# Self-attention on one Trainium2 core: values of two pairs of heads projected together

## What is computed

```python
def _L0_attn_ref(x, Wq, Wkv, Wo, bo, rel_emb):          # x is already normed: (2, 1024, 256)
    q = (x @ Wq).reshape(b, n, h, d).transpose(0, 2, 1, 3)
    kv = x @ Wkv
    k, v = jnp.split(kv, 2, axis=-1)
    ...
    dots = jnp.einsum('bhid,bhjd->bhij', q, k) * scale
    dots = dots + _rel_bias(rel_emb, n)[None]
    attn = jax.nn.softmax(dots, axis=-1)
    out = jnp.einsum('bhij,bhjd->bhid', attn, v)
    out = out.transpose(0, 2, 1, 3).reshape(b, n, h * d)
    return out @ Wo + bo
```

## Time and profile before

| | |
|---|---|
| median of 3 runs | 2049.24 us (2044.33 to 2055.61) |
| the profiled execution | 2053.66 us, span 2051.9 us |
| self-attention loop, first to last scores' block | about 58 to 901 us of the span |
| PE / DVE / ACT / POOL busy, share of the span | 91% / 63% / 47% / 47% |
| mean granted clock of TensorE | 0.959 of full |

### The profile page before, as it was taken

The page is one execution under the profiler, slowest core; times in us unless marked ns, Lnnn a source line. Parts: engine busy times, 40 slices in busy tenths (PEclk is TensorE's granted clock), DMA queues, the critical chain, the costliest instruction groups (busy, mean ns, idle before and its releaser), DMA issues.

```text
span 2051.9 us, 52537 instructions
## 1 busy us (share of the span) xinstructions
PE 1871.6 (91%) x21476; PEld 1552.1 (76%) x21476; DVE 1301.8 (63%) x2932; ACT 973.9 (47%) x1984; POOL 967.1 (47%) x783
## 2 busy tenths in 40 slices
PE   7999999999999999987559489999999999988994
PEld 5677777777777777765447389999899999987873
DVE  6667676767676766647756565555565554556883
ACT  3666666666666666533136043334343443335451
POOL 2555555555555555545633733334234334435440
PEclk9999999999999999999869699999999999999996
DMA  6101020101230100234133520000220000220000
GB/s 246 50 19 47 19 78 19 50 19 70 101 129 19 50 12 12 70 133 130 47 135 126 155 78 13 23 13 13 79 80 26 19 18 18 85 73 16 15 14 16
DMA packets 74606, 119.85 MB, mean 58 GB/s; under 512 B 8392, under 2 KB 64464, under 8 KB 70992
## 3 DMA queue, kind: packets, MB, share of 16 engines
q1 hardware_dynamic: 69392, 105.31, 15.3%
q0 software_dynamic: 2560, 6.30, 1.1%
q10 hardware_dynamic: 2416, 4.88, 0.6%
HBM read 76.61 MB, written 39.85 MB: 57 GB/s over the span
## 4 chain that ended last, share of the span: by engine, by line
PE 41%; DVE 5%; POOL 3%; issue 2%; DMA 2%; ACT 2%; SPq 1%; POOLq 0%; DVEq 0%; ACTq 0%
PE psum L265 12%; PE psum L276 9%; PE psum L2019 4%; PE psum L2007 2%; PE psum L2511 2%; PE psum L1993 2%; PE psum L225 1%; PE psum L2545 1%; PE psum L1367 1%; PE psum L1350 1%; POOL b_yg L1484 1%; PE psum L246 1%; ACT e_pr L2650 1%; PE psum L1260 1%; PE psum L2520 1%
## 5 line engine op out<-in xcount | busy, mean ns | idle before, releaser
L774 POOL TENSOR_TENSOR a_sm<-a_sm,a_rsum 128x1024 f32<-128x1024 f32 x256 | 479.8, 1893 | 357.5 <-DVE a_rsum L808 355.1
L796 DVE CUSTOM_DVE_ANT_0 a_sm<-psum,a_strip 128x1024 f32<-128x1024 f32 x256 | 312.0, 1219 | 146.8 <-PE psum L628 146.8
L709 ACT ACTIVATE a_sm<-a_sm,a_mn 128x1024 f32<-128x1024 f32 x256 | 293.9, 1148 | 28.2 <-DVE a_mn L796 26.9
L714 ACT ACTIVATE a_pT<-psum 128x512 f32<-128x512 f32 x256 | 151.5, 592 | 273.1 <-PE psum L641 273.1
L641 PE MATMUL psum<-ident,a_sm 128*128 128x128 f32 x2048 | 275.2, 277 | 5.2 <-POOL a_sm L774 4.2
L641 PEld LDWEIGHTS psum<-ident,a_sm 128*128 128x128 f32 x2048 | 223.8, 140 | 62.7 <-issue 46.0
L656 PE MATMUL psum<-a_pT,a_V 128*64 128x256 f32 x2048 | 249.0, 385 | 0.6 <-ACT a_o L720 0.6
L656 PEld LDWEIGHTS psum<-a_pT,a_V 128*64 128x64 f32 x2048 | 136.1, 136 | 77.3 <-issue 22.1
L803 DVE COPY a_pT<-psum 128x512 f32<-128x512 f32 x256 | 174.8, 683 | 12.1 <-PE psum L641 4.9
L2103 ACT ACTIVATE g_val<-psum 128x512 f32<-128x512 f32 x64 | 38.0, 596 | 225.0 <-PE psum L2019 225.0
L628 PE MATMUL psum<-a_KH,a_QH 64*128 64x512 f32 x512 | 114.8, 445 | 2.5 <-DVE a_mn L796 2.5
(11 more groups left out here) (396 smaller groups left out, 3736.2 us busy)
## 6 DMA issues: line engine op xcount, KB each, us to landing
a_strip<-table SPq DMA_DIRECT2D x16, 960.0 KB, 6.7
oT<-a_o SPq DMA_DIRECT2D x64, 128.0 KB, 1.9
xs<-b_zeros SPq DMA_DIRECT2D x8, 1024.0 KB, 4.1
b_oT_in<-oT SPq DMA_DIRECT2D x7, 1024.0 KB, 5.9
y<-b_yb SPq DMA_DIRECT2D x23, 256.0 KB, 2.2
b_xs<-xs SPq DMA_DIRECT2D x23, 128.0 KB, 2.2
a_raw<-in_a_wqkv SPq DMA_DIRECT2D x7, 384.0 KB, 3.3
s_x<-in_x_rev SPq DMA_DIRECT2D x4, 512.0 KB, 8.0
```

Of the source, the lines that this page charges most:

```text
L709: a.activation(sm[:, st % RING, :], sm[:, st % RING, :], ACT.Exp, scale=-1.0, bias=mn[:, at:at + 1], accum_out=rsum[:, at:at + 1]).then_in ...
L714: a.activation(probs(st, 0), psum[:, 4, :].rearrange("p (k q) -> p k q", k=4), ACT.Copy).then_inc(sig("pT_act"), 1)
L774: g.tensor_tensor(sm[:, st % RING, :], sm[:, st % RING, :], rsum[:, at:at + 1].broadcast_to([P, T]), ALU.mult).then_inc(sig("scaled"), 1)
L796: v.tensor_tensor_reduce(out=sm[:, st % RING, :], in0=scores_banks(hl).rearrange("p c n -> p (c n)"), in1=strip[:, pair % 2, hl, qt * P:qt ...
```

## The change

Values of an even pair and of the odd pair after it are projected in one unit. The stationary operand is still a tile of tokens; the moving operand is the values' weights of both pairs side by side, 256 columns, and the three passes are accumulated in the same columns (12 matmuls of 256 columns, no 128-column ones, no second partial sum). ACT copies the even pair's columns into a buffer of its own, `Vs[0]`, which lies where the next stage's first slot will be loaded; DVE copies the odd pair's columns into `Vs[1]` (a copy where an addition was).

A block of an even pair has 8 units, one of an odd pair only its 4 k and q units. These are put at tiles 0, 2, 3 and 5 of the block before it; tiles 1, 4, 6 and 7 have no unit. `split(1)` is moved ahead of the loop, since the first v unit needs both pairs' weights, and its raw load ahead of the strips; the later splits and raw loads are moved to match.

```diff
-        Ws = [sb(f"W{r}", [P, 2, KC, 3 * P], F32R, lies=32) for r in range(2)]
+        W_pair = sb("W", [P, 2, 2, KC, 3 * P], F32R, lies=32)
+        Ws = [W_pair[:, r, :, :, :] for r in range(2)]
...
-        V = sb("V", [P, B, KT, P])
+        Vs = [nc.alloc_sbuf_tensor_at("a_V_even", [P, B, KT, P], F32, offset=early["wo_at"] + HP * D * 4), sb("V", [P, B, KT, P])]
...
-        parts = [("k", 0), ("k", 1), ("q", 0), ("q", 1)] + [("v", c) for c in range(KT // 2)]
-        NU = len(parts)
-        ACT_V = NU - 4
-        units = [(pair, b, what, c) for pair, b in blocks for what, c in parts]
+        both = [("k", 0), ("k", 1), ("q", 0), ("q", 1)]
+        parts = [both + [("v", c) for c in range(KT // 2)], both]
+        NU, NQK = len(parts[0]), len(both)
+        units = [(pair, b, what, c) for pair, b in blocks for what, c in parts[pair % 2]]
+        base = [sum(len(parts[pair % 2]) for pair, _ in blocks[:i]) for i in range(len(blocks) + 1)]
+        unit_at = {}
+        for i, (pair, _) in enumerate(blocks[1:]):
+            for u, n in enumerate(range(KT) if pair % 2 == 0 else (0, 2, 3, 5)):
+                unit_at[i * KT + n] = base[i + 1] + u
...
+        split_at = {2 * KT * (pair - 1 - pair % 2) + (KT if pair % 2 else 2): pair for pair in range(2, HP)}
...
+                load_raw(1)
                 load_strips(0)
-                load_raw(1)
                 load_strips(1)
...
-                    if g % 8 == 2 and pair + 2 < HP:
-
+                    if g % 8 == 2 and pair % 2 == 0 and pair + 2 < HP:
                         sp.wait_ge(sig("w_lo"), pair + 1)
                         load_raw(pair + 2)
+                        load_raw(pair + 3)
...
+                    if (what, c) == ("v", 0):
+                        pe.wait_ge(sig("w_lo"), pair + 1)
...
-                            for k in range(KC):
-                                pe.matmul(bank[:, t * 2 * P:(t + 1) * 2 * P].rearrange("p (s n) -> p s n", s=2), hT[0][:, k, tile],
-                                          W[:, :, k, 2 * P:3 * P], start=k == 0, stop=False)
-                            for k in range(KC):
-                                last = pe.matmul(bank[:, t * 2 * P:t * 2 * P + P], hT[1][:, k, tile], W[:, 0, k, 2 * P:3 * P],
-                                                 start=False, stop=k == KC - 1)
+                            out = bank[:, t * 2 * P:(t + 1) * 2 * P].rearrange("p (s n) -> p s n", s=2)
+                            for i, (ws, hs, k) in enumerate(terms):
+                                last = pe.matmul(out, hT[hs][:, k, tile], W_pair[:, :, ws, k, 2 * P:3 * P],
+                                                 start=i == 0, stop=i == len(terms) - 1)
...
-                    if n < tail:
-                        project(NU + n)
-                    else:
+                    if n in unit_at:
+                        project(unit_at[n])
+                    elif n >= tail:
                         first["tensor"](pe, n - tail)
...
-                        last = a.activation(V[:, b, 2 * c:2 * c + 2, :], bank.rearrange("p (t s n) -> p t s n", t=2, s=2)[:, :, 0, :], ACT.Copy)
+                        last = a.activation(Vs[0][:, b, 2 * c:2 * c + 2, :], bank.rearrange("p (t s n) -> p t s n", t=2, s=2)[:, :, 0, :], ACT.Copy)
...
+                split(1)
                 for u in range(NU):
                     project(u)
...
-                        rows = V[:, b, 2 * c:2 * c + 2, :]
-                        last = v.tensor_tensor(rows, rows, bank.rearrange("p (t s n) -> p t s n", t=2, s=2)[:, :, 1, :], ALU.add)
+                        last = v.tensor_copy(Vs[1][:, b, 2 * c:2 * c + 2, :], bank.rearrange("p (t s n) -> p t s n", t=2, s=2)[:, :, 1, :])
```

More of the change, by code:

```diff
@@ L644, in values @@
                 def values(g, half):
-                    _, b, _ = tiles[2 * g]
+                    pair, b, _ = tiles[2 * g]
                     if half == 0:
@@ L649, in values @@
                         pe.wait_ge(sig("pT_dve"), 4 * (g + 1))
-                        pe.wait_ge(sig("proj_out"), NU * (2 * g // KT + 1))
+                        blk = 2 * g // KT
+                        pe.wait_ge(sig("proj_out"), base[blk - 2 * (pair % 2)] + NU)
                         if g:
@@ L655, in values @@
                             rows = slice(hl * DH, (hl + 1) * DH)
-                            last = pe.matmul(bank_o[rows, 0:GQ], V[:, b, kt, rows], pT[:, g % 2, hl, kt, :],
+                            last = pe.matmul(bank_o[rows, 0:GQ], Vs[pair % 2][:, b, kt, rows], pT[:, g % 2, hl, kt, :],
                                              start=kt == 0, stop=kt == KT - 1)
@@ L665, in project @@
                         pe.wait_ge(sig("proj_out"), u)
-                    if u % (2 * NU) == 0 and pair:
+                    if (what, c) == ("k", 0) and pair:
                         pe.wait_ge(sig("w_lo"), pair)
+                    if (what, c) == ("v", 0):
+                        pe.wait_ge(sig("w_lo"), pair + 1)
                     terms = passes(KC)
@@ L722, in project @@
                 def project(u):
-                    _, b, what, c = units[u]
+                    pair, b, what, c = units[u]
+                    blk = 2 * pair + b
                     bank = unit_bank(u)
@@ L727, in project @@
                     if what == "k":
-                        if u % NU == 0 and u >= 2 * NU:
-                            a.wait_ge(sig("scores"), 2 * KT * (u // NU - 1))
+                        if c == 0 and blk >= 2:
+                            a.wait_ge(sig("scores"), 2 * KT * (blk - 1))
                         last = a.activation(KH[:, b, c * CH:(c + 1) * CH], bank, ACT.Copy)
@@ L733, in project @@
                     else:
-                        if u % NU == ACT_V and u >= 2 * NU:
-                            a.wait_ge(sig("o_ps"), KT // 2 * (u // NU - 1))
-                        last = a.activation(V[:, b, 2 * c:2 * c + 2, :], bank.rearrange("p (t s n) -> p t s n", t=2, s=2)[:, :, 0, :], ACT.Copy)
+                        if c == 0 and blk >= 2:
+                            a.wait_ge(sig("o_ps"), KT // 2 * (blk - 1))
+                        last = a.activation(Vs[0][:, b, 2 * c:2 * c + 2, :], bank.rearrange("p (t s n) -> p t s n", t=2, s=2)[:, :, 0, :], ACT.Copy)
                     last.then_inc(sig("proj_hi"), 1)
@@ L741, in split @@
                     if pair > 1:
-                        a.wait_ge(sig("proj_ps"), 2 * NU * (pair - 1))
+                        a.wait_ge(sig("proj_ps"), base[2 * (pair - 1)])
                     a.activation(Ws[pair % 2][:, 0, :, :], raws[pair % 2][:, :, :], ACT.Copy).then_inc(sig("w_hi"), 1)
+                split(1)
                 for u in range(NU):
@@ L757, in _ @@
                         exps(2 * n + 3)
-                    if NU + n < len(units):
-                        project(NU + n)
-                    else:
+                    if n in unit_at:
+                        project(unit_at[n])
+                    elif n >= tail:
                         first["scalar"](a, n - tail)
-                    if n % (2 * KT) == 2 and n // (2 * KT) + 1 < HP:
-                        split(n // (2 * KT) + 1)
+                    if n in split_at:
+                        split(split_at[n])
                 stored(NG - 2)
@@ L853, in _ @@
                     emptied(2 * n + 1)
-                    if n % (2 * KT) == 3 and n // (2 * KT) + 1 < HP:
-                        split(n // (2 * KT) + 1)
+                    if n - 1 in split_at:
+                        split(split_at[n - 1])
     for signals in old:
```

8 lines of the change are left out of this document (4 added, 4 removed).

## The result

Four runs of the changed kernel lie between 2057.85 and 2065.43 us, median **2062.68 us**. The four runs of the kernel before that stand beside them have a median of 2047.94 us. The ratio is 1.0063 with a 95% interval of [1.0038, 1.0088]: **0.63% slower**, which is 12.9 us on 2047.94 (7.8 to 18.0 us by the interval); the medians are 14.7 us apart. Forecast were 2061.8 us and +12.6. The profiled execution took 2057.85 us, with a span of 2056.1 us at a mean granted clock of 0.96.

A forecast was written before the change was run, and what follows sets the result against it. PE's work bounds a tile only above a floor near 6.16 us, set by reuse of banks 4 and 5. Terms 13.6 + 1.9 - 2.9 = +12.6 us on the 2049.24 median gave 2061.8 us; range 2050 to 2068.

The forecast's parts named there:

- A v unit becomes longer: Attention loop: 12 matmuls replace 8, +0.487 us per unit with nothing to cover it, +13.6 us for 28 units.
- Half of the v units go: Attention loop: 32 tiles left without a unit fall only from 6.25 to the 6.16 us floor, -2.9 us.
- k and q units are moved: Odd pairs' blocks in the loop: units change tiles but keep number and length, 0 us.
- DVE, ACT, SP: Loop: fewer V operations on DVE and ACT, moved splits and paired raw loads on SP cost nothing, 0 us.
- The start: Ahead of the loop: four longer v units add +1.9 us; the earlier split costs 0, its low weights covered by 1.3 us.
- The sum: Whole kernel: 13.6 + 1.9 - 2.9 = +12.6 us, for a median of 2061.8 us, 0.61% slower.
- PE's work is the limit: Rival, 32 empty tiles: each saves its 0.96 us, -15.2 us in all, 2034.0 us; chance 7%.
- POOL is late in addition: Rival, two empty tiles in a row: PE waits for probabilities POOL must scale, +1.7 to +6.7 us, up to 2068.5; 8%.
- A cheaper 256-column matmul: Rival, v units: at 0.110 us per matmul the sum is +9.6 us, 2058.8 us, no change that can be told; 9%.
- The low weights late: Rival, start: low weights of pair 1 come late, +2.0 us, 2063.8 us; chance 5%.
- The later stages take the delay in: Rival, the 1150 us behind the loop: up to all of the 12.6 us is lost there, 2049 us; chance 9%.

The follow-up runs named there:

- third experiment: The changed kernel with the low tokens' pass left out of its v unit, 8 matmuls of 256 columns instead of 12: 2055.09 us, ratio 0.999 to the kernel before.
- second experiment: The changed kernel's order, but even pairs keep the old 8-matmul v unit and odd pairs' values are not computed: 2050.04 us, ratio 0.9966 to the kernel before.
- first two experiments: One is the kernel before with the low tokens' pass left out of each v unit: 2050.33 us, ratio 0.9971; the other is the second experiment.
- seventh experiment: The changed kernel with k0 and q0 halved over two tiles, and empty tiles 6 and 7 writing bank 7 first, bank 4 second: 2057.11 us, ratio 1.0002.
- eighth experiment: The changed kernel with the raw weights of pair 1 loaded behind the four strips, not ahead of them: 2076.26 us in one run.
- spare bank for ACT: The changed kernel with the half of the second transposes that ACT empties put into bank 7 in empty tiles: 2068.68 us, ratio 1.005 to the kernel before.
- sixth experiment: The changed kernel with odd pairs' k0 and q0 each cut into 3 + 3 matmuls over two tiles: 2062.74 us, ratio 1.0022 to the kernel before.
- fourth experiment: The changed kernel with the half of the second transposes that DVE empties put into bank 7 in empty tiles: 2061.14 us, ratio 1.0025 to the kernel before.

## Why the prediction was right

**A v unit becomes longer: +0.487 us each, measured 0.54 to 0.56.** The mechanism held: nothing in the tile covers the excess. The term was mis-sized mostly in the gap at the unit's edge, put at 0.03 us for old and new alike. The third experiment shows 0.08 us once and 0.120 per matmul, so 12 x 0.120 + 0.08 = 1.52 us, against 0.96 for the old one, for which 0.03 holds. The second experiment gives 15.1 us for the 28 units instead of 13.6. The distance itself, 0.118 from the earlier trace rows, was 0.002 low. That a load of weights sets this distance was inferred from equal paces and not tried.

The formula in the Trainium skill, page "TensorE: Matmul & The Clock Gate", section "Back-to-back issue gap", by which it would be 0.109, is given there for a single matmul, not for a stream of loads and matmuls. The trace does not agree with it for this stream, which loads 128x128 weights before each matmul. The prediction put it in for the new unit alone and got about +9 us; put in for the old unit too, it makes that 4 x 0.109 + 4 x 0.056 = 0.66 us and the sum about +18 us, an estimate from the page's figures.

**Half of the v units go: -2.9 us.** Held: 6.25 to 6.16 in all 32 tiles, and -3.75 us in the loop when done alone, 0.5 of it from two long tiles of before. This was the step that decided the sign. The experiments with a spare bank correct its working: it named both banks, and at this floor only bank 5, DVE's, counts. PE's wait for ACT comes before it and is hidden.

**k and q units are moved: 0.** Held: behind the first block k and q tiles take 6.73 to 6.77 us in both kernels. **DVE, ACT, SP: 0.** Held, with what covers the split on DVE now known: cut the unit beside it in half and the block pays 0.3 us.

**The start: +1.9 us, measured +1.59.** The v units took 5.84 us instead of 3.74, which is +2.10. Against that the k and q units, which start 0.37 us later, end 0.51 us earlier: from 44.70 to 58.00 the mean granted clock was 0.87 against 0.81. This is luck and not the change's doing, as far as these traces tell: in the second experiment, with the change's order at the start, the same units take 7.92 us, against 6.97 in the change and 7.85 before. The rows:

```profile
45.08 0.36 SPq L586 DMA_DIRECT2D a_raw<-in_a_wqkv  x1
...
49.38 0.85 ACT L752 ACTIVATE a_W<-a_raw 128x768 fp32r<-128x768 f32 x1 [7.00 <-DMA a_raw<-in_a_wqkv]
...
50.26 0.96 DVE L838 TENSOR_TENSOR a_W<-a_raw,a_W 128x768 fp32r<-128x768 f32 x1 [6.40 <-ACT a_W L752]
...
52.09 0.64 PE L689 MATMUL psum<-a_W,a_hT_hi 128*128 128x256 f32 x4
```

The low weights were ready at 51.22, as forecast (51.3), but by two errors that cancelled: the load was issued and landed later, so that ACT's split began at 49.38 instead of 48.4, and DVE's split took 0.96 us instead of 2.05. The profile of before had a row for that: pair 0's split, at 33.99 with POOL idle, took 0.95 us. PE asked at 52.09, so 0.87 us of cover were left, of the 1.3 forecast.

**The sum: +12.6 us, measured +12.92** at the loop's end in the profiled pair, +12.9 by the ratio and +14.7 between the medians. That it came within 0.3 us is partly luck, for the terms were further off than their sum: the longer unit cost 1.5 us more in the loop, the empty slots gave back 0.85 more, and the start took 0.3 less. It is luck as well that 2061.8 lies 0.9 us from the median, with runs of the kernel before spread over 11 us.

**The rivals.** *PE's work is the limit* fell with the empty tiles at 6.16 and with the first two experiments. *POOL is late in addition* did not show in the change: its empty tiles all stand for the banks. A wait for it appears one step further on, in the seventh experiment. *A cheaper 256-column matmul* fell with the 0.120 us. *The low weights late* did not occur; the eighth experiment shows that its price would have been above the wait alone. *The later stages take the delay in* needs all runs together: how far the 121st tile's first transposes stand from 843.13 in each profile, and how far the kernel's time is from that of before beside it:

| kernel | loop's end, us | by the ratio, us | by the medians, us |
|---|---|---|---|
| shorter unit in before | -8.37 | -6.0 | -5.9 |
| the change without its heavier unit | -4.29 | -7.0 | -6.2 |
| two passes | -2.39 | -2.1 | -1.2 |
| halves and spare bank | -1.50 | +0.4 | +1.9 |
| halves | +4.11 | +4.5 | +7.5 |
| spare bank for DVE | +5.81 | +5.1 | +4.9 |
| the change | +12.92 | +12.9 | +14.7 |
| spare bank for ACT | +12.95 | +10.3 | +13.5 |
| raw load behind the strips (one run) | +23.61 | - | +21.0 |

Over 32 us both columns of times follow the first within 3.4 us. A line through them rises by about 0.9 us per us, give or take 0.2 (an estimate from the table), so by the times alone a fifth of the delay could be lost unseen, but not the greater part. The profiles say more: from the 121st tile to the end of the span nine of the ten take 1207.8 to 1214.6 us, 1211.2 where the loop ends first and 1207.8 where it ends last, 32 us later, and only the change's takes 1200.1. A delay at the loop's end is passed on in the main; the 8.7 us of the one profiled pair are scatter of the stages behind it. What makes them scatter was not tried.

## What to carry to other kernels

Before work is merged into fewer, heavier pieces, find a place in the trace of before where the freed slot is already empty, and read its length: if the loop has a floor there, emptied slots are worth only the distance to it, while every heavier slot pays in full. A PE that reads 100% busy can hide such a floor, since a wait within a group of matmuls lengthens the group instead of showing as idle; compare the durations of equal groups (1.06 against 1.33 us here). Work below the floor should be spread evenly: three 512-column matmuls in an empty tile were free here, except where another engine's work, DVE's split, stood in the same tile.

## What was not expected of the hardware

- DVE's split (128x768, both inputs in SBUF) took 0.96 us at the start with POOL's product absent, but 2.05 us in the loop and 2.28 in the sixth experiment. There POOL's product runs from 190.51 to 192.40, and the split, started at 190.94, ends at 193.22, 0.82 us after POOL: as if it had stood until POOL was done. So it is with every split in the loop, of 2.05 or 2.28 us, in before, in the change and in the sixth experiment: each begins while a product of POOL is under way and ends 0.81 to 0.82 us after it. By the Trainium skill, page "SBUF — State Buffer", section "SBUF: two separate sides", a VectorE operation with two SBUF inputs and a GpSimd operation lock a shared pair of ports for a whole instruction, and the later one is blocked; the traces agree with it, in these durations.
- After 8.24 us without a matmul PE's next stretch ran at a granted clock of 0.50, the lower of its two levels (1.2 and 2.4 GHz), up to 65.20, and 48 matmuls took 8.10 us instead of 5.84. A wait of 1.76 us was followed by such a fall in the third and the fourth experiment (a mean of 0.66, and 1.2 us more), but the same wait of 1.75 us in the change was not.
- The same 384 KB load was in use 4.30 us after its issue when issued first (45.08 to 49.38), and 11.70 us when issued behind the strips (46.77 to 58.47); four strips of 960 KB each were issued beside it both times.
